# A two-layer convolution and state-space kernel: SiLU by one function over several strips, and a block's products and a bf16 split moved to GpSimd

## The reference

```python
# layer 0: two scan directions, a state of 32 x 64 for each of 12 heads
xl, z = split(x @ W_in.T)                      # 384 + 384 channels
xc = silu(depthwise3x3(xl) + conv_b)
B, C, dt = xs @ x_proj.T ; dt = softplus(dt + dt_bias)
h = exp(dt * A) * h + dt * x * B ; y = h . C + D * x       # per token
out = x + (y0 + y1) * silu(z) @ W_out.T
out = out + silu(out @ W1.T + b1) @ W2.T + b2
# layer 1: half of the channels through three convolutions, half through a selective scan
xi, zz = split(layernorm(xr) @ in_proj.T)      # 192 + 192 channels
xi = silu(depthwise3x3(xi) + conv2d_b)
delta = softplus(dts @ dt_proj.T + bias)       # 4 directions, 192 channels
h = exp(delta * A) * h + (delta * u) * B ; y = h . C       # state of 16 for each channel
xr_out = (layernorm(y0 + y1 + y2 + y3) * silu(zz)) @ out_proj.T
out = interleave(xl_out, xr_out) + x
```

## Time and profile before

| | |
|---|---|
| time, median of 3 runs | 19261.31 us (19232.4 to 19284.86) |
| the profiled execution | 19287.62 us, of it span 19285.8 us |
| share of the span | PE 76%, DVE 82%, ACT 43%, POOL 53% |
| first scan to last scan of a middle round | 2217 us of a round of 2291 us |
| granted TensorE clock | 0.826 of full speed |

### The profile page before, as it was taken

How to read it: one execution, slowest core, us unless ns; L and a number is a source line. 1 busy time by engine, 2 the same in 40 slices (tenths; PEclk the granted TensorE clock), 3 DMA queues, 4 the chain that set the end, 5 groups by cost and what they waited for, 6 DMA issues and landing times. The chain is left out here.

```text
span 19285.8 us, 212341 instructions
## 1 busy us (share of the span) xinstructions
PE 14729.8 (76%) x65784; PEld 6341.4 (33%) x65784; DVE 15816.2 (82%) x12143; ACT 8249.6 (43%) x14280; POOL 10174.2 (53%) x5172
## 2 busy tenths in 40 slices
PE   7886789677886788767886878867788678874554
PEld 4433433233332333234332343324333233321102
DVE  3327989689887988979888798988988798898994
ACT  3244334543355334643346433454335533463332
POOL 2115755466455654547455574456645565454662
PEclk9988888788988889888977888878898888975555
DMA  2226666566765667666675666666766566757774
GB/s 80 85 75 174 179 180 168 162 174 186 176 167 166 180 180 187 169 163 182 170 194 163 170 183 177 176 172 174 189 175 167 169 179 180 188 166 175 185 183 113
DMA packets 1556889, 3220.31 MB, mean 167 GB/s; under 512 B 289936, under 2 KB 721872, under 8 KB 1554256
## 3 DMA queue, kind: packets, MB, share of 16 engines
q1 hardware_dynamic: 1555792, 3206.72, 62.4%
HBM read 2474.94 MB, written 731.12 MB: 166 GB/s over the span
## 5 line engine op out<-in xcount | busy, mean ns | idle before, releaser
L1887 POOL TENSOR_TENSOR HC<-H,BR 128x1024 f32<-128x1024 f32 x3072 | 7380.3, 2404 | 5919.5 <-DVE H L1738 3717.3
L1738 DVE TENSOR_TENSOR_SCAN H<-dA,CR,PU 128x1024 f32<-128x1024 f32 x2304 | 5400.1, 2344 | 375.9 <-ACT CR L1119 166.8
L789 PE MATMUL PU<-PT,SELB 96*128 96x512 bf16 x6144 | 2280.3, 460 | 3097.3 <-DVE H L1738 2536.4
L1119 ACT ACTIVATE dA<-dA,A 128x1024 f32<-128x1024 f32 x3072 | 3508.6, 1143 | 2306.2 <-DMA dA<-dld 2280.4
L1482 DVE TENSOR_TENSOR PU<-PU,BR 128x1024 f32<-128x1024 f32 x3072 | 3731.2, 1215 | 411.5 <-PE PU L789 390.3
L789 PE MATMUL PB<-RA,RB 128*128 128x64 f32 (+3 forms) x9120 | 2804.8, 456 | 76.2 <-DVE RA L1485 65.1
L789 PE MATMUL PY<-HC,CB 128*32 128x256 f32 x24576 | 2397.2, 469 | 72.0 <-POOL HC L1887 51.2
L789 PEld LDWEIGHTS PU<-PT,SELB 96*128 96x128 bf16 x6144 | 505.2, 104 | 4675.4 <-issue 4065.7
L1738 DVE TENSOR_TENSOR_SCAN H<-dA,PU 128x1024 f32<-128x1024 f32 x768 | 1755.0, 2285 | 141.1 <-ACT dA L1119 49.3
L789 PEld LDWEIGHTS PB<-RA,RB 128*128 128x128 f32 (+2 forms) x9120 | 1394.6, 188 | 1307.7 <-issue 1173.8
L789 PE MATMUL PB<-RA 128*128 128x384 f32 (+2 forms) x4272 | 1758.1, 551 | 9.0 <-ACT RA L1119 9.0
(11 more groups left out here) (174 smaller groups left out, 18145.8 us busy)
## 6 DMA issues: line engine op xcount, KB each, us to landing
dA<-dld SPq DMA_DIRECT2D x3072, 512.0 KB, 6.4
PT<-ptd SPq DMA_DIRECT2D x2304, 64.0 KB, 4.4
BR<-bcd SPq DMA_DIRECT2D x256, 512.0 KB, 7.4
ptd<-RA SPq DMA_DIRECT2D x176, 576.0 KB, 3.9
y0d<-RA SPq DMA_DIRECT2D x512, 192.0 KB, 7.8
RA<-y0d SPq DMA_DIRECT2D x128, 768.0 KB, 6.5
yd<-YS SPq DMA_DIRECT2D x768, 128.0 KB, 4.9
tkd<-RB SPq DMA_DIRECT2D x256, 262.0 KB, 4.8
```

What stands on the lines that cost most here:

```text
L789: return nc.tensor.matmul(out, w, x, start=start, stop=stop, skip_group_check=True)
L1119: return ac.activation(out, in_, f, **kw)
L1738: v.tensor_tensor_scan(h, a, x, 0.0 if first else K.CR[:, gi:gi + 1], MUL, ADD).then_inc(S["s_scan"], 1)
L1887: po.tensor_tensor(K.HC[:, w % NHC, :], K.H[:, w % NH, :], K.BR[:, (w // 24) % NBR, 1, :], MUL).then_inc(S["s_mulC"], 1)
```

## The change

1. **SiLU.** The halved weights, tanh and the product on DVE go. ACT takes the function Silu in place over several strips at once: three strips in phase a (128 x 1536, 8 a round), the six of the MLP (128 x 3072, 8 a round), both of z (96 x 1024, 8 a round), and four of the second convolution (96 x 2048, 4 a round). The strips of the MLP and of z are first written from PSUM by one ACT instruction each (bias added) instead of two. The convolutions' sums are kept in larger buffers: `TA`, made of T0 and T1, in phase a, and C1 in phase e. xc0 is written by one DMA for three strips, zd by one for two.
2. **b_mix.** ACT copies C B^T from PSUM to SBUF (GS, 128 x 128) and POOL multiplies EE by it; DVE's instruction goes.
3. **Split.** The first and second parts are the upper 16 bits of the f32 words (`upper`, every second bf16 of the bits), not a rounded copy. POOL takes both subtractions, E1 = E0 - upper(E0) and part 3 = E1 - upper(E1); ACT copies upper(E0) and upper(E1), both strided. E0 has 3 buffers and E1 3, where E0 had 4. SP waits for all three parts.
4. **The written order.** All tables of kinds first and middle are new. In a middle round DVE's steps now fall so: a in slots 0 to 49, b in 49 to 153, c in 153 to 234, d with h in 234 to 303, e in 303 to 344, f from 344 on; behind the last slot stand 64 steps of DVE, 74 of POOL, 65 of ACT and 61 of PE, all of phase f. In the second round b takes slots 73 to 189, c 189 to 283, f starts at 372, and behind the last slot stand 105 steps of DVE, 45 of POOL, 40 of ACT and 38 of PE. The last kind is as before.

```diff
-NR, NE, NX = 10, 4, 4
+NR, NE, NX = 10, 3, 4
@@ 
+def upper(t):
+
+    return t.bitcast(BF)[..., 1::2]
@@ ACT
+    def a_silu(m, p):
+        i, j = divmod(m, 3)
+        if p or j < 2:
+            return
+        ac.wait_ge(*R.at("half", m + 1, "a"))
+        if i:
+            ac.wait_ge(S["a_tproj"], 4 * i)
+            ac.wait_ge(S["xj"], 16 * i)
+        act(K.XJS, K.TA[i % 2], ACT.Silu).then_inc(S["silu"], 1)
@@ ACT
+    def b_mix(u, p):
+        ac.wait_ge(S["b_g"], u + 1)
+        if u >= 2:
+            ac.wait_ge(S["b_mix"], u - 1)
+        act(K.GS[u % 2], R.bank(("b.mix", u, 0))[:, 0:128], ACT.Copy).then_inc(S["b_gs"], 1)
@@ ACT, c_mlp
-        act(K.MA[m % 2], pb[:, :], ACT.Tanh, bias=K.DV0[:, 18 + j:19 + j], scale=0.5)
-        act(K.MB[m % 2], pb[:, :], ACT.Identity, bias=K.DV0[:, 18 + j:19 + j], scale=0.5).then_inc(S["c_hact"], 1)
+        act(K.HB[i % 2][:, strip(j)], R.bank(("c.mlp", i, j))[:, :], ACT.Identity,
+            bias=K.vec("b1", j, P=128)).then_inc(S["c_hact"], 1)
+        if j == 5:
+            ac.wait_ge(S["c_hact"], m + 1)
+            act(K.HB[i % 2], K.HB[i % 2], ACT.Silu).then_inc(S["c_hs"], 1)
@@ DVE: a_silu, b_mix, c_mlp, e_inproj, e_silu go; f_split
-            v.wait_ge(S["f_sum"], u + 1)
-            v.wait_ge(S["f_p0"], u + 1)
-            tt(e, e, K.PP[u % 3][:, 0, :], SUB).then_inc(S["f_x1"], 1)
@@ POOL
+    def b_mix(u, p):
+        po.wait_ge(S["b_exp"], 2 * u + 2)
+        po.wait_ge(S["b_gs"], u + 1)
+        if u >= 2:
+            po.wait_ge(S["b_y"], u - 1)
+        po.tensor_tensor(K.MM[u % 2].rearrange("p (h t) -> p h t", h=6), K.EE[u % 2].rearrange("p (h t) -> p h t", h=6),
+                         K.GS[u % 2].unsqueeze(1).to_broadcast([128, 6, 128]), MUL).then_inc(S["b_mix"], 1)
@@ POOL, f_split
+        e0, e1 = K.E0[u % NE], K.E1[u % NE]
+        if part < 2:
+            po.wait_ge(S["f_sum"], u + 1)
+            if u >= NE:
+                po.wait_ge(S["f_p1"], u - NE + 1)
+                po.wait_ge(S["f_x2"], u - NE + 1)
+            po.tensor_tensor(e1, e0, upper(e0), SUB).then_inc(S["f_x1"], 1)
+        else:
+            po.wait_ge(S["f_x1"], u + 1)
+            if u >= 3:
+                po.wait_ge(S[f"pp{u % 3}"], 16 * (u // 3))
+            po.tensor_tensor(K.PP[u % 3][:, 2, :], e1, upper(e1), SUB).then_inc(S["f_x2"], 1)
```

More of the change, by code:

```diff
@@ L417, in emptied @@
     if name == "b.mix":
-        return [("b_mix", i + 1)]
+        return [("b_gs", i + 1)]
     if name == "b.out":
@@ L472 @@
            "g_y13 g_all h_n h_g h_gate h_mm h_copy "
-           "rim diag taps side conv tap half tanh silu mean xm sq var vr rstd").split()
+           "rim diag taps side conv tap half silu mean xm sq var vr rstd").split()
 DMAS = {"weights": None, "xt0": None, "xt1": None,
-        "xin0": None, "xin1": None, "xj0": {"a": 128}, "xj1": {"a": 128}, "xj2": {"a": 128},
+        "xin0": None, "xin1": None, "xj": {"a": 128},
         "tko0": {"a": 256}, "tko1": {"a": 256},
@@ L660, in __init__ @@
         self.HF = [rb(384, 32) for _ in range(2)]
+        self.GS = [rb(128) for _ in range(2)]
         ra, rb = both()
[L664 removed]
+        self.HB = [ra(3072), PX[:, :]]
         self.YG = [ra(512) for _ in range(3)]
@@ L1297, in e_side, with e_silu @@
         ac.wait_ge(S["e_rows"], 2 * min(i + 1, 7) + 2)
-        side_taps("e", m, 96, K.YP[:, j], 27 + 9 * j, K.DV0[0:96, 24 + j:25 + j], i)
-    def e_conv(m, tap):
-        if tap == NTAP:
-            if m == 0:
-                ac.wait_ge(S["e_p"], 32)
-            conv_tanh("e", m, 96)
+        if m == 0:
+            ac.wait_ge(S["e_xn"], 8)
+        side_taps("e", m, 96, K.C1[:, j, strip(i)], K.YP[:, j], W1 + 9 * j, K.vec("cdb", j), i)
+    def e_silu(m, p):
+        j, i = divmod(m, 8)
+        if i % 4 == 3:
+            x = K.C1[:, j, (i - 3) * 512:(i + 1) * 512]
+            ac.wait_ge(*R.at("half", m + 1, "e"))
+            act(x, x, ACT.Silu).then_inc(S["silu"], 1)
     def f_begin(_, p):
@@ L1785, in h_gates @@
             tt(o, o, K.ZB[:, strip(j)], MUL).then_inc(S["h_gate"], 1)
-    do = {"a.begin": a_begin, "a.conv": a_conv, "a.silu": a_silu, "b.setup": b_setup, "b.mix": b_mix, "b.out": b_out,
-          "c.begin": c_begin, "c.gate": c_gate, "c.outp": c_outp, "c.mlp": c_mlp, "c.mlp2": c_mlp2,
-          "d.begin": d_begin, "e.begin": e_begin, "e.mean": e_mean, "e.norm": e_norm, "e.inproj": e_inproj,
-          "e.conv": e_conv, "e.silu": e_silu, "f.begin": f_begin, "f.split": f_split, "s": s_slot,
+    do = {"a.begin": a_begin, "a.conv": a_conv, "b.setup": b_setup, "b.out": b_out,
+          "c.begin": c_begin, "c.gate": c_gate, "c.outp": c_outp, "c.mlp2": c_mlp2,
+          "d.begin": d_begin, "e.begin": e_begin, "e.mean": e_mean, "e.norm": e_norm,
+          "e.conv": e_conv, "f.begin": f_begin, "f.split": f_split, "s": s_slot,
           "g.total": g_total, "g.mean": g_mean, "h.gates": h_gates}
```

429 lines of the change are left out of this document (188 added, 241 removed), and 3 rows, old and new, of the table SHARED.

## The result

The changed kernel takes 18,959.4 us (median of 4 runs, 18,911.56 to 18,973.87) against 19,265.8 us of the kernel before on the same chip: a ratio of 0.984, 95% interval 0.9815 to 0.9861, 1.6% faster. The forecast was 18,943 us.

The account below looks back on a forecast made before the run. DVE was taken to bound b, d and e, PE a and c, with DVE and POOL excluding each other in f. From 19,288 us: -282 (middle rounds), -67 (second), +30 (first) give 18,969; median 18,943, range 18,480 to 19,330.

Parts of the forecast that it names:

- What DVE loses: In a middle round the edits take 221 us of DVE's 1983; the round gets only 47 us shorter.
- a, c, d, e: Phases of a middle round: a 312 us (now 320), c 415 (396), d 385 (375), e 212 (227).
- b: Phase b of a middle round: the bound moves from DVE to POOL, at 90%; 565 us, now 664.
- f and the rest: Phase f and behind the last slot: DVE and POOL exclude each other, 6.2 us a unit; 354 us, now 308.
- Second round: The round after the start: gains in b, d and e, losses in c, a and f, together -67 us.
- First round: The start without a scan: f gets +20 us and b +10, so +30 us.
- ACT's table sets: Silu's 28 calls cost ACT two loads each, 72 us a round, hidden; priced at 0, upper end 56 a round.
- rival 3: On ACT, Silu calls hold dA and the scan waits: 56 us a round, 392 in all; 19,250 to 19,335; chance 0.08.
- The sum: Middle round 2243 us, 47 less than 2290; profiled execution 18,969 us, median 18,943.
- 1: In phase b POOL isn't the bound and waits stay rare: product 1.47 us, b 512, total 18,500 us; chance 0.22.
- 2: In f and behind the last slot, strided bf16 makes POOL's subtractions 3.1 us each; total 19,400 us, slower; chance 0.14.
- 4: The SiLU and b_mix edits leave DVE on the path because PE leads, 2060 us; binds in a and c alone.

## Why the prediction was right, and where it was not

*What DVE loses*, 221 us a round: the durations of its instructions sum to 215 us less, and the windows, which count overlapping ones once, go from 1983 to 1786, 197 less (1760 was forecast). The step stands. Of it 47 us were forecast to reach the round's time; 37.5 do.

*a, c, d, e*: right to 8 us each. e is 8 us over, 12 in the mean of the six middle rounds; without the table loads, which were priced at 0, it is 9 less in that mean.

*b* is the step that failed: "the bound moves from DVE to POOL", at 90% and 565 us. The loads on both engines were right (POOL 498 against 504, DVE 471 against 458, product 1.81 against 1.84). But at 594 us neither bounds it. Halving the product gave nothing, shortening the token loads gave 49 us, and halving it then gave 26 more. The new order puts 35 of the 64 blocks in slots 60 to 96, nearly one a slot where it was one in two, while a load is issued 11 us after its buffer is free and lands 11 us after that. The forecast summed engines alone, and had no term for the loads. Before, the load showed only in the first round, where b runs at its own pace and PE waited 47.8 us for it; it was not looked at there.

*f and the rest*: 354 forecast, 320 measured. The serial cost of a unit was taken as 6.2 us; the tail (what stands behind the last slot) takes 5.5 for a unit whose product stands there too. One such stretch on POOL (start, length):

```profile
7995.42 1.89 POOL L1859 TENSOR_TENSOR RA<-RA 96x1024 f32<-96x1024 f32 x1
7997.27 1.89 POOL L1859 TENSOR_TENSOR PX<-RA 96x1024 f32<-96x1024 f32 x1
7999.12 3.60 POOL L1864 TENSOR_TENSOR RA<-RA 96x1024 bf16<-96x1024 f32 x1
8002.68 3.59 POOL L1864 TENSOR_TENSOR RA<-PX 96x1024 bf16<-96x1024 f32 x1
```

Two subtractions at 1.89, two at 3.6 with DVE's product inside them, 11 us for two units. The mechanism (DVE and POOL exclude each other) was right, the term 1.9 + 2.2 + 2.1 was mis-sized by 0.7 us, 0.5 of it in POOL's two. Besides, four of the 19 units of the tail had their product before it: the 19 took 96 us where 118 were forecast, 22 of the 34. The rest lies in the 43 slots, 186 us for 200.

*Second round*: -67 forecast, -78 measured. *First round*: +30 forecast, -41 measured, the wrong sign. b did not move (+10 forecast): PE waits 48 and 46 us for tokens on both sides, and in the kernel after short loads take 30 us from it; a ended 24 us earlier where the forecast had taken no gain without a scan; the splits took 158 us (1301.0 to 1459) against 169 (1332.0 to 1500.9), not 20 more.

*ACT's table sets*: 56 loads more a round forecast, 49 measured in a middle round (68 for 19), each 1.283 us. Their price is 72 us in the run, not 0, and not rival 3's 392.

The Trainium skill (page "ScalarE: Activation LUTs", What ACT_TABLE_LOAD costs) gives about 2.66 us a switch, of which 1.283 are the load and the rest a drain: by an estimate from that page the 340 loads added over the run would be 904 us of ACT. The rows agree on the load, 1.283 us each or 436 us in all, and show no drain behind it; the measurement decides.

*The sum*: the middle round's errors, -2, +29, +8, +1, +8, -34 us, leave +10 here and +9.5 in the mean of six, 57 us less gain than forecast; the first round's 71 us go the other way and the second's 11. By these the profiled execution should come 25 us below its forecast of 18,969, and is 21 below. The median was then put 26 us below the profiled execution and lies 12 above it, which brings the forecast to 16 us below the measured median. That the total is right to 16 us is chance; the parts are right to about 30 us a round.

*The rivals*: 1 was right that POOL is not the bound in b, but for another reason and with the other sign: its product near 1.47, its rare waits and its b of 512 us did not come. 2 had a premise that holds for another tile (0.22 us) and not for this one. 3 was right in sign at a fifth of its price, and not by its wait for dA. 4 was right for a and c.

## What to carry to other kernels

When work leaves the engine that bounds a stage, ask of the stage's loads too at what pace they can follow: where they stand in the issuing engine's order, how long they take to land, and whether they ever wait for a buffer. Here the new pace came from the loads, and from neither of the two engines whose sum had been made; and since no load waited for its buffer, more buffers under the same order would not have brought one forward. Halve the work that is thought to bind: no change is a clear answer, and repeating it after the suspected limit is lifted shows the second limit. When a wait grows after an edit, look for the one that shrank: it may only have changed hands. A forecast by stages should be read by stages: here the middle round was right to 10 us because two errors of some 30 us cancelled.

## What the runs showed of the hardware

- POOL's subtraction of bf16 from f32, 96 x 1024, undisturbed: 1.88 us when the bf16 are the upper halves of the very words of the first input, 2.11 with a contiguous bf16 tile, 2.33 with every second bf16 of another tile.
- Such an instruction takes 3.6 us where DVE's product of two SBUF tiles starts beside it, 1.7 us more, as before the change.
- Tanh lies in a set with Exp, Silu in none with Exp (473 loads in all with Silu, 109 with Tanh in the same calls).
- With short token loads the granted clock in b rose from 0.85 to 0.91 (means over stretches at 2.4 GHz and at 1.2; in the 37 dense slots it was 1.00, 2.4 GHz throughout), and PE's own busy time fell from 435 to 408 us for the same 2839 matmuls.
- A 512 KB load of dA landed in 10.3 us (median) in b, and in 5.4 once the token loads beside it were short, while the DMAs moved 168 and 165 GB/s.
